# Early rows added behind the last tile or in attention, result stores issued by ScalarE, in a macaron block of mixture-of-experts, attention and mixture-of-experts

## What is computed

```python
x = x + 0.5 * ffn(layernorm(x))
x = x + attn(layernorm(x))
x = x + 0.5 * ffn(layernorm(x))        # the same weights again

def ffn(x):                            # 32 experts, each 256 -> 128 -> 256
    scores = softmax(x @ gate_weight.T)
    # the 3 best of 8 groups of 4 experts, then the 6 best experts in them,
    # their scores divided by their sum: combine, [2048, 32]
    y = sum(combine[:, e] * ((silu(x @ w1[e].T) * (x @ w3[e].T)) @ w2[e].T) for e in range(32))
    return y + (silu(x @ sw1.T) * (x @ sw3.T)) @ sw2.T      # shared expert, 256 wide
```

## Time and profile before

| | us |
|---|---|
| runs | 975.6, 956.46, 954.28 |
| median | 956.46 |
| the profiled execution | 960.5 |
| its span, from the first instruction to the last | 958.7 |

### The profile page before, as it was taken

How to read it: one execution, slowest core, us unless ns; L and a number is a source line. 1 busy time by engine, 2 the same in 40 slices (tenths; PEclk the granted TensorE clock), 3 DMA queues, 4 the chain that set the end, 5 groups by cost and what they waited for, 6 DMA issues and landing times. The chain is left out here.

```text
span 958.7 us, 16120 instructions
## 1 busy us (share of the span) xinstructions
PE 772.8 (81%) x4554; PEld 609.0 (64%) x4555; DVE 513.0 (54%) x1439; ACT 358.5 (37%) x799; POOL 465.3 (49%) x487
## 2 busy tenths in 40 slices
PE   6895997999969789788889575686999995867486
PEld 6464885888847546576677374564888884645154
DVE  5774942434313537888887469672444431135274
ACT  3160443444424314465665224233444442322000
POOL 3005665553053335867754320655555406456884
PEclk9979898999988898999999755688999998887798
DMA  6862465643233463222220140233444413334524
GB/s 209 338 286 77 158 214 176 231 164 120 89 121 114 159 227 89 80 76 67 72 62 2 34 176 1 77 121 120 153 158 154 138 77 121 126 112 131 207 82 153
DMA packets 42358, 126.43 MB, mean 132 GB/s; under 512 B 8352, under 2 KB 16704, under 8 KB 39488
## 3 DMA queue, kind: packets, MB, share of 16 engines
q1 hardware_dynamic: 23872, 75.40, 20.7%
q0 software_dynamic: 18432, 50.36, 18.0%
HBM read 76.44 MB, written 49.28 MB: 131 GB/s over the span
## 5 line engine op out<-in xcount | busy, mean ns | idle before, releaser
L399 POOL DMA_INDIRECT back<-token_table,slots x192 | 186.7, 973 | 221.9 <-DVE slots L644 96.3
L911 PE MATMUL bank<-w,xt 128*128 x1024 | 260.7, 400 | 33.2 <-ACT xt L492 18.4
L911 PEld LDWEIGHTS bank<-w,xt 128*128 128x128 f32 x1024 | 196.5, 200 | 69.4 <-issue 44.2
L420 POOL DMA_INDIRECT back<-slot_table,combine x124 | 130.0, 1049 | 143.6 <-SPq L328 42.2
L690 DVE TENSOR_TENSOR mids<-mids,bank 128x256 f32<-128x256 f32 x128 | 53.8, 420 | 256.6 <-ACT mids L469 197.3
L931 PE MATMUL bank<-w,mids 128*128 x512 | 142.9, 405 | 4.5 <-DVE mids L697 2.6
L492 ACT COPY xt<-ring 128x256 f32 x256 | 91.5, 408 | 104.0 <-issue 75.9
L931 PEld LDWEIGHTS bank<-w,mids 128*128 128x128 f32 x512 | 93.2, 203 | 16.0 <-issue 7.1
L469 ACT ACTIVATE mids<-bank 128x256 f32<-128x256 f32 x128 | 49.0, 383 | 145.2 <-PE bank L911 87.8
L680 DVE COPY ring<-bank 128x512 f32 (+1 forms) x96 | 66.1, 689 | 46.6 <-PE bank L901 31.2
L923 PE MATMUL bank<-const,mids 128*128 128x128 f32 x256 | 52.6, 290 | 45.7 <-DVE mids L690 24.2
(11 more groups left out here) (209 smaller groups left out, 1070.9 us busy)
## 6 DMA issues: line engine op xcount, KB each, us to landing
slot_table<-gT SPq DMA_DIRECT2D x32, 512.0 KB
slot_table<-ey SPq DMA_DIRECT2D x32, 512.0 KB
w<-in_w SPq DMA_DIRECT2D x12, 1024.0 KB, 17.1
slot_table<-w SPq DMA_DIRECT2D x6, 1024.0 KB
token_table<-back SPq DMA_DIRECT2D x8, 512.0 KB, 2.9
back<-token_table,slots POOLq DMA_INDIRECT x192
x<-in_x SPq DMA_DIRECT2D x4, 512.0 KB, 5.7
turn_a<-in_turn SPq DMA_DIRECT2D x4, 512.0 KB
```

The costliest lines, as they stand in the source:

```text
L399: pool.indirect_dma_start(out=rows[q % RX][:, a * H:(a + 1) * H], out_offset=None, in_=table, in_offset=bass.IndirectOffsetOnAxis(ap=slots ...
L420: pool.indirect_dma_start(out=returned[g % len(returned)], out_offset=None, in_=y_table, in_offset=bass.IndirectOffsetOnAxis(ap=combine[:, ...
L911: last = nc.tensor.matmul(bH[u % 2][:, a * 2 * I:(a + 1) * 2 * I], xt[u % 2][:, a * H + k * P:a * H + (k + 1) * P], w13[:, bass.ds(expert[ ...
```

## The change

Six tiles of weights are dead before the pairs end: once the pairs of experts 0 to 5 are done, `w13[:, 0:6 * WE]` and `w2[:, 0:6 * H]` are no longer read in this layer. They are cut into 18 more buffers for returned rows (`spared`), so that there are 34 in the first layer and 46 in the second. At the end of attention SP loads these weights again for the second layer. The second layer's buffers of the shared expert move behind them, and the columns of all tokens come in four loads into parts of the ring that are no longer read.

- ScalarE issues the store itself, behind the result copy of u = 1 and of u = 3, after a wait for that copy. SP only waits for landings, in order, and counts 4 tiles more for each.
- A column is released when its last tile has landed (`end`, no longer `end + 4`). The waits that spaced the gathers of the first layer are gone; one wait for the pairs of the first six experts stands in front of the first spared buffer.
- No row is added within the pairs. In the first layer VectorE adds column n = 0 behind the last pair and leaves n = 1 in its buffers; attention adds it first in each tile, five adds a tile (ADDS) instead of four. In the second layer all 96 adds follow the last pair.
- SP loads the columns for the shared expert eight pairs before the end.

```diff
+GONE = 6
 REST = TOPK - EARLY
+ADDS = REST + EARLY - 1
...
+        spared = [part[:, i * H:(i + 1) * H] for part, n in ((w13, GONE * WE // H), (w2, GONE)) for i in range(n)]
+        s_early = [sem(f"s_early{n}") for n in range(EARLY)]
...
-                    returned = [part[:, i * H:(i + 1) * H] for part, n in ((back, NT), (s1, KS * TB // H))
-                                for i in range(n)]
+                    returned = [back[:, i * H:(i + 1) * H] for i in range(NT)] + spared
...
+                    again = [ring[:, a:a + KC * TB] for a in (spare, spare + KC * TB, SPAN + spare, 0)]
+                    returned = [back[:, i * H:(i + 1) * H] for i in range(KEEP)] + spared
...
-                        def store(it, u):
-                            m = it * RY + u
-                            sp.wait_ge(e_y, done + m * 2 + 2)
-                            sp.dma_start(y_table.rearrange("(p t) h -> p t h", t=ST)[:, bass.ds(m * 4, 4), :],
-                                         y[u].rearrange("p (t h) -> p t h", h=H)).then_inc(s_yst[u], 16)
-                            if f == 1 or u > 0:
-                                sp.wait_ge(s_yst[(u - 1) % RY], (it + f * (NQ // 2 // RY) + (u > 0)) * 16)
-                            else:
-                                sp.wait_ge(s_yst[(u - 1) % RY], it * 16)
+                        def landed(it, u):
+
+                            sp.wait_ge(s_yst[u], (it + f * (NQ // 2 // RY) + 1) * 16)
                             sp.sem_inc(s_there, 4)
...
+                        sp.wait_ge(e_h, done + NQ - EDGE)
...
+                            for it in range(T // TB):
+                                sp.dma_start(again[it].rearrange("p (k t) -> p k t", k=KC), stored[:, it]).then_inc(s_again[it], 16)
...
                             end = pool.value_load(last_of_column[k:k + 1, 0:1], min_val=1, max_val=ST)
-                            hold(pool, s_there, end + 4, s_held)
+                            hold(pool, s_there, end, s_held)
...
+                                if g == (KEEP if f else NT):
+                                    pool.wait_ge(e_h, done + GONE * NT // 2)
+                                    pool.wait_ge(e_yp, done + GONE * NT // 2)
                                 if g >= len(returned):
                                     pool.wait_ge(s_add, g - len(returned) + 1)
-                                if f == 0 and g % 2 == 0:
-                                    pool.wait_ge(e_h, NQ - NT - 3 + g // 2)
...
                             nc.scalar.copy(y[u // 2][:, u % 2 * 2 * H:(u % 2 + 1) * 2 * H], bY[u % 2][:, :]).then_inc(e_y, 1)
+                            if u % 2:
+                                act.wait_ge(e_y, done + q + 1)
+                                act.dma_start(y_table.rearrange("(p t) h -> p t h", t=ST)[:, bass.ds((lap * RY + u // 2) * 4, 4), :],
+                                              y[u // 2].rearrange("p (t h) -> p t h", h=H)).then_inc(s_yst[u // 2], 16)
...
-                        with dve.Fori(0, (NQ - EDGE - NP) // 2) as it:
+                        with dve.Fori(0, (NQ - NP) // 2 - 1) as it:
                             pairs(it * 2 + NP, 2)
-                        pairs(NQ - EDGE, EDGE, final=True)
+                        pairs(NQ - 2, 2)
                         copy_mid(NQ - 1, NQ - 1)
-                        if f == 1:
...
+                        if f == 0:
+                            for i in range(NT):
+                                add_row(0, i, 0, 2 * len(its))
+                        else:
...
+                            add_rows(0, 0)
                             product(0)
+                            add_rows(1, 0)
                             product(1)
-                            dve.wait_ge(s_add, 4 * NT)
-                            shared_of(0, 2)
-                            add_rows(4)
+                            shared_of(0, 2, 2)
+                            add_rows(2, 2)
                             product(2)
-                            dve.wait_ge(s_add, 5 * NT)
-                            shared_of(2, 4)
+                            shared_of(2, 4, 3)
                             product(3)
-                            add_rows(5, 0, NT // 2)
-                            shared_of(4, 8)
-                            add_rows(5, NT // 2, NT)
+                            add_rows(3, 4)
+                            shared_of(4, 8, 4)
+                            add_rows(4, 8)
+                            add_rows(5, 8)
...
+                        sp.wait_ge(add_ok, NT * ADDS)
+                        sp.dma_start(w13[:, 0:GONE * WE], w13_in[:, 0:GONE * WE]).then_inc(s_big, 16)
+                        sp.dma_start(w2[:, 0:GONE * H], w2_in[:, 0:GONE * H]).then_inc(s_big, 16)
...
-                                    dve.wait_ge(back_ok[j % RB], (j // RB + 1) * REST * 16)
+                                    dve.wait_ge(s_early[1], NT * 16)
...
+                                if k == 1:
+                                    dve.wait_ge(back_ok[j % RB], (j // RB + 1) * REST * 16)
+                                row = back[j % RB][:, (k - 1) * H:k * H] if k else spared[i]
```

More of the change, by code:

```diff
@@ L272, in moe @@
                 columns = TOPK if f else EARLY
-                s_back = [sem(f"s_back{k}") for k in range(columns)]
+                s_back = [sem(f"s_back{k}") for k in range(columns)] if f else s_early
                 s_last = [sem(f"s_last{q}") for q in range(4)] if f else []
@@ L715, in shares, with add_row @@
                             ch(nc.vector.tensor_reduce(v3(share[:, :], TOPK)[:, :, k], v3(equal[:, :], E), AX.X, ALU.add))
-                        def add_row(n, i):
+                        def add_row(n, i, before, shared):
                             k, g = TOPK - 1 - n, n * NT + i
@@ L732, in add_row, with pairs @@
                                 x[:, i * H:(i + 1) * H], ALU.mult, ALU.add).then_inc(s_add, 1)
-                        def pairs(q0, n, at=None, first=False, final=False):
+                        def pairs(q0, n, at=None, first=False):
                             for i in range(n):
@@ L808, in logits, with shared_in @@
                             last.then_inc(s_lg, 1)
-                        def shared_in(it, tokens):
+                        def shared_in(it):
+                            if f == 0:
+                                tokens = [xnT[:, k * T + its[it] * TB:k * T + (its[it] + 1) * TB] for k in range(KC)]
+                            else:
+                                tokens = [again[it][:, k * TB:(k + 1) * TB] for k in range(KC)]
+                                pe.wait_ge(s_again[it], 16)
                             if it == 0:
@@ L1563, in rows_of @@
                         def rows_of(j):
-                            for k in range(REST):
+                            for k in range(ADDS):
                                 add_rows(k)(j, j % B)
@@ L1600, in _ @@
                         shifted_mean(3, 1)
-                        for k in range(1, REST):
+                        for k in range(1, ADDS):
                             add_rows(k)(4, 0)
```

86 lines of the change are left out of this document (40 added, 46 removed).

## The result

The changed kernel is slower: 1014.8 us (median of 4, 1006.3 to 1027.6) against 956.9 for the kernel before in the same comparison, a ratio of 1.058 with a 95% interval of 1.051 to 1.065. The ratio leaves out the longest execution of each kernel (1027.6 and 975.6 us), which ran in a slower state. Forecast were 1006.2, range 972 to 1032.

The account below looks back on a forecast made before the run. TensorE's expert matmuls and ScalarE's turn once a lap were taken to bound the pairs, GpSimd's gathers the tail. Terms 29.4 + 1.7 + 3 + 15.6 = 49.7 us on the median 956.46 gave 1006.2, range 972 to 1032.

Parts of the forecast that it names:

- Turns: Load of ring columns at each lap's top: ScalarE's store ahead delays it 1.05 us, 28 turns counted, 29.4 us.
- signs named: Steady laps 14.7 us against 13.7, ScalarE's gap 3.7, TensorE's wait 1.5, DMA issue about 0.33 on ScalarE.
- The load itself may be a little quicker there: ScalarE's load at the turn, of varying length, might shorten; delay taken as 1.05 us instead of 1.17.
- Stalls at 0: TensorE's unexplained idle stretches in each layer's last pairs: no term for them in the sum.
- longer stalls: Rival, last pairs: stalls last as long as their gather runs, TensorE loses 10 us more per layer; about 1026; chance 0.22.
- Barrier and attention: After the first layer's pairs: attention starts 1.7 us later, and 16 more adds in attention cost 3 us.
- Tail: After the second layer's last pair: 50 gathers remain instead of 40, five add runs slow them; together +15.6 us.
- Full exclusion: Rival: each add beside gathers stops them for its whole 0.40 us, 12.8 us instead of 5.2; 1014; chance 0.06.
- the 56 gathers: Second layer: gathers issued before VectorE's first add at 886.8 in the kernel before; the change stops GpSimd at 46 buffers.
- Stalls gone: Rival, last pairs: mid-run gather waits and adds between pairs cause the stalls; ending both regains 57 us, 949; chance 0.10.

Follow-up runs that it names:

- first, longer execution: First profiled execution of the changed kernel, its longest of the first comparison: 1027.6 us, span 1025.7.
- narrow adds: Changed kernel with the second layer's adds of expert rows working on one column of 256: 1015.0 us, 1.048 of the kernel before.
- first group: Quiet-chip comparison, kernel before 884.9 us: changed kernel with SyncE issuing stores again, 882.1; kernel before with only ScalarE's stores and SyncE's arrival count, 910.9.
- second execution: Changed kernel unaltered, profiled in a later comparison: span 1014.5, 1016.3 us in all; that comparison measured 1021.0 us, 1.056 of the kernel before.

## Why the prediction was right, and where it was not

- **Turns: right in size and place.** Forecast 28 of 1.05, 29.4 us. Traced: 11.7 and 8.7 in the steady pairs of the two layers and, at 1.1 each, about 4.4 for the four turns in each layer's last pairs, 29.2. That it meets the forecast so closely is partly luck: behind the 8.7 stand two first laps, with stalls in both kernels, that took 1 us less together and not 2 more, and in pairs 45 to 63 on the quiet chip the kernel with ScalarE's stores and spaced gathers takes 8.0 and 3.6 us more than the one with SyncE's stores and free gathers (63.6 against 55.6, 62.4 against 58.8). The stores alone on a quiet chip: 26.0. The signs named were there (gap 3.7, TensorE's wait 1.5, DMA issue 0.34).
- **"The load itself may be a little quicker there": wrong.** It is 2.55 us against 2.51. I had read its varying length as noise or queueing. At the turns it has two usual lengths, 1.76 without and 2.5 to 2.6 with a store just issued (up to 4.0 with the stores back on SyncE), and in the kernel before SyncE's store stood beside it as well. This didn't hurt the sum, for both kernels pay it. It hid a good edit: 0.7 us a lap in the kernel before. The Trainium skill (Runtime: NRT & Kernel Launch, section Instruction fetch mechanics) gives a load of registers from HBM about 200 ns per register. An estimate from that for eight values is 1.6 us, near the 1.76 measured here without a store, though this table lies in SBUF.
- **Stalls at 0: the step that failed.** I kept them as they were and gave "longer stalls" 0.22. Traced: 9.7 + 11.5 less 8.8 of turns, 12.4 us more, and by the same account 19.8 in the first, longer execution (16.5 + 12.1 less 8.8). With the turns at the 11.6 just named it is some 3 us less. The rival's mechanism was right: a stall lasts with the run of gathers, and the change took away the wait that spaced them. Its price (20) was nearer than my 0. My argument against it was that 40 gathers of the tail ran without a stall. With narrow adds the tail stalls too. That slow gathers beside full adds break up the runs is not the whole reason: in the kernel before 17 quick gathers stand in one run there (893.8 to 915.3), and the product that TensorE ended beside the 13th (909.24) was taken up at 909.28. So a long run is not enough by itself, and what else it takes is open. My row reading was off as well: two of the six stalls stand beside runs of 10 and 11 gathers, not 12 to 16.
- **Barrier and attention: 4.7 forecast.** From pair 63 to the second layer's pair 0, routing included, it is 0.5 in the first execution and 2.7 in the second, and 3.3 between the two kernels of the first group on the quiet chip. The direction is right, the size somewhat high.
- **Tail: 15.6 forecast, 13.6 and 14.2 traced.** Fifty gathers in 78.8 us (forecast 77). A run of 16 adds costs GpSimd 3.3 us beside these gathers, where I took 2.6. Full exclusion would be 6.4 a run and 32 for the five; 16.4 were lost. So the full exclusion that I took from the Trainium skill (SBUF — State Buffer, Who interferes with whom) again shows only in part: some gathers pass, one in about ten is held.
- **What lies under the tail was not seen.** I took the 56 gathers that the kernel before has issued by its last pair as given. They are a fruit of the stalls: GpSimd goes on while TensorE stands. On the quiet chip, where it does not stand, the 46 buffers nearly suffice (3.2 us of pause instead of 34), and the tail is 4.0 us longer than in the kernel before with ScalarE's stores (90.1 against 86.1) and not 13.6. So of stalls and tail, some 26 of the 56 us, all but 4 belong to the chip as much as to the change; the 26 to 29 of the stores do not.
- **"Stalls gone" (949)** named adds and broken runs as their cause. VectorE's adds left the last pairs and the stalls stayed, so that part is refuted; breaking the runs shortened the stalls.
- The sum was 49.7. On the second execution it is -2.0 + 29.2 + 12.4 + 2.7 + 13.6 = 55.9, and the medians differ by 58. The miss is the stalls, 12.4, less 6 us that the tail, the attention and the start took below the forecast.

**Open.** Why a run of gathers delays TensorE's word to the others is not settled. The records show that the signals come late while TensorE goes on, that beside the pairs runs of eight gathers or more do it and runs of about four hardly, and that two of the chips don't do it at all with the same gathers at the same 1.25 us. Neither the path of the signals nor what differs between the chips shows in these traces. One difference does show, and it raises a rival that no run tests. Take the kernel with gathers in eights: on the quiet chip 6 of 2642 semaphore updates by computing instructions have no record of their own within 0.3 us of the instruction's end; on the chip with stalls it is 447, of TensorE, VectorE and ScalarE, in steady laps too. Most of these signals must have come in time, for the laps there are as short; it is their records that are missing. The other kernels divide in the same way, at most 10 on the quiet chips and over 300 on the chip with stalls. Every execution on record carries the profiler's span and clock, so it may be the recording itself that holds TensorE up on that chip. No execution without it is on record, and this stays open. Free gathers with the store behind the turn were not run on a chip with stalls, nor gathers in twos in both layers.

## To carry to other kernels

Before you move a DMA issue to a busy engine, find the one point per loop where another engine waits for it, and put the issue just behind that point: the same stores cost 26 us with one of two ahead of the turn and nothing with it behind. Look also at what is issued while a sequencer loads values, since a store beside it made that load 0.8 us longer, whoever issued it. And where gathers on GpSimd run beside matmuls and TensorE stalls without a reason in the rows, try them in runs of about four: in the first layer pauses of 1.5 us saved 19 to 26 us on the chip with stalls and cost nothing on a quiet one, where in the second layer, whose gathers the end waits for, they cost 10.

## What the hardware did that I had not expected

- A load of eight values by ScalarE's sequencer takes 1.76 us, and 2.5 to 2.65 (medians) when a 512 KB store was issued up to half a microsecond before or beside it.
- The same kernel takes 884 us on two chips and 963 to 970 on a third. For the kernel with gathers in eights, 59 of the 72 us between a quiet chip and that one lie in the stages of the pairs, nearly all in laps beside runs of gathers, of token rows as well as of results. Up products are signalled 16 and 24 us late there, and the granted clock is lower (0.74 to 0.86 in pairs 45 to 63 with free gathers, 1.00 on the quiet chips).
- On that chip 32 gathers cost the first layer's last pairs 2.5 us in runs of two to six, 12 in runs of eight, and 22 to 28 in runs of about sixteen.
- The store behind the turn with free gathers is 0.974 of the kernel before on a quiet chip; with the gathers in runs of eight it is 0.984 on a quiet one and 0.983 on the other kind. Which is best on a chip with stalls isn't shown.
